# Attention stage of a two-layer decoder: one TensorE tile shape of 64 rows by 32 columns, two value banks, two score banks

## The reference

```
q = _layernorm(q, q_gamma, q_beta)
k = _layernorm(k, k_gamma, k_beta)
logits = jnp.einsum('bhsd,bhtd->bhst', q, k) / (math.sqrt(Dh) * T)
att = jax.nn.softmax(logits, axis=-1)
out = jnp.einsum('bhst,bhtd->bhsd', att, v)
```

## Time and profile before

| | |
|---|---|
| runs | 1680.69, 1681.13, 1683.37 us |
| median | 1681.13 us |
| span of the profiled execution | 1681.4 us (no other time of it is shown) |
| TensorE clock granted | mean 0.994 of full speed |
| busy: TensorE / VectorE / ScalarE / GpSimd | 1598.4 / 1499.6 / 1319.1 / 406.3 us |
| attention stage | about 130 to 1253 us of the span |

### The profile page before, as it was taken

The page is one execution under the profiler, slowest core; times in us unless marked ns, Lnnn a source line. Parts: engine busy times, 40 slices in busy tenths (PEclk is TensorE's granted clock), DMA queues, the critical chain, the costliest instruction groups (busy, mean ns, idle before and its releaser), DMA issues. The chain is left out here.

```text
span 1681.4 us, 36595 instructions
## 1 busy us (share of the span) xinstructions
PE 1598.4 (95%) x14449; PEld 634.1 (38%) x14452; DVE 1499.6 (89%) x2182; ACT 1319.1 (78%) x2590; POOL 406.3 (24%) x666
## 2 busy tenths in 40 slices
PE   6999999999999999999999999999989999889997
PEld 3542222222223232223322222222235555657774
DVE  6899999989999999989899999999948887688876
ACT  4618999879988989898899999999985565545544
POOL 5800110212223312312211111111013443533302
PEclk9999999999999999999999999999999999999999
DMA  4001001001101200101221011010002000015551
GB/s 147 14 7 20 14 14 14 14 14 22 31 14 21 45 14 14 33 17 27 70 55 26 14 21 20 14 27 14 14 28 63 1 1 1 1 31 95 101 102 51
DMA packets 148026, 52.32 MB, mean 31 GB/s; under 512 B 137424, under 2 KB 146128, under 8 KB 147600
## 3 DMA queue, kind: packets, MB, share of 16 engines
q1 hardware_dynamic: 147152, 48.62, 14.1%
q10 hardware_dynamic: 704, 1.38, 0.2%
HBM read 14.07 MB, written 2.10 MB: 10 GB/s over the span
## 5 line engine op out<-in xcount | busy, mean ns | idle before, releaser
L968 DVE TENSOR_REDUCE mxp<-ps_m 128x2 f32<-128x1024 f32 (+2 forms) x928 | 1049.3, 1198 | 41.3 <-PE ps_m L747 39.9
L897 ACT ACTIVATE work<-ps_s 128x512 f32<-128x512 f32 x1856 | 1001.7, 598 | 76.7 <-PE ps_s L771 48.9
L797 PE MATMUL ps_av<-work,vst 128*32 128x256 f32 x7424 | 592.8, 391 | 14.7 <-ACT avs L904 12.3
L771 PE MATMUL ps_s<-qb,k_stack 50*128 50x512 f16 x1856 | 565.8, 382 | 0.5 <-ACT v_rows L915 0.3
L747 PE MATMUL ps_m<-k_stack,qa 48*128 48x512 f16 (+1 forms) x2048 | 534.1, 358 | 2.3 <-PEq L1123 0.5
L797 PEld LDWEIGHTS ps_av<-work,vst 128*32 128x32 f32 x7424 | 147.0, 108 | 383.2 <-ACT work L897 321.6
L771 PEld LDWEIGHTS ps_s<-qb,k_stack 50*128 50x128 f16 x1856 | 119.7, 94 | 378.6 <-ACT work L897 323.4
L747 PEld LDWEIGHTS ps_m<-k_stack,qa 48*128 48x128 f16 x2048 | 108.2, 93 | 21.5 <-DVE mxp L968 14.8
L616 POOL TENSOR_SCALAR mtmp<-negm 128x16 f32<-128x16 f32 x32 | 8.2, 255 | 390.5 <-DVE negm L973 390.4
L602 POOL COPY vst<-v_rows 128x1024 f32<-128x1024 f32 (+1 forms) x32 | 30.6, 956 | 144.5 <-PE ps_av L797 144.5
L682 POOL TENSOR_TENSOR q_rows<-avs,rc 128x256 f32<-128x256 f32 x31 | 19.2, 619 | 173.3 <-DVE rc L979 173.3
(11 more groups left out here) (441 smaller groups left out, 2006.1 us busy)
## 6 DMA issues: line engine op xcount, KB each, us to landing
x_res<-in_x SPq DMA_DIRECT2D x4, 512.0 KB, 8.2
w_experts<-in_w_experts SPq DMA_DIRECT2D x1, 2048.0 KB, 8.0
out<-x_res SPq DMA_DIRECT2D x8, 256.0 KB, 2.2
v_rows<-in_ctx_c SPq DMA_DIRECT2D x1, 1664.0 KB, 7.3
work<-in_ctx_t SPq DMA_DIRECT2D x1, 1456.0 KB, 15.8
ctx_n<-in_ctx_n SPq DMA_DIRECT2D x1, 1248.0 KB, 8.0
w_qkv<-in_w_qkv ACTq DMA_DIRECT2D x1, 768.0 KB, 8.6
w_qkv<-in_w_qkv SPq DMA_DIRECT2D x1, 768.0 KB, 4.2
```

The costliest lines, as they stand in the source:

```text
L771: pe.matmul(ps_s[:, bank, :], STACKS[part(n)][rows, group(n) * PAIRS + j, t * P:t * P + P], qb[n % 2][rows, :, j, :], start=True, stop=Tru ...
L797: m = pe.matmul(ps_av[32 * h:32 * h + 32, cols], vst[n % 2][:, t, h, :], pbuf[(tau[n] + t) % 2][:, h, cols], start=(t == 0 and half == 0), ...
L897: a.activation(pbuf[g % 2][:, h, :], ps_s[:, b, :], ACT.Exp, scale=factor).then_inc(s["exp"], 1)
L968: v.tensor_reduce(dst, src, AX.X, ALU.max).then_inc(s["mred"], 1)
```

## The change

Scores, maxima and values all use tiles of 64 rows by 32 columns. A score is four matmuls with 32 keys each; a side of a maximum unit is four with 32 queries each; a value product is split into keys 0 to 63 and 64 to 127 (`side`), which go to two banks of `ps_av`. `collect` copies both banks (1024 columns) to `raw`, which lies in the same memory as `spare`, and a new step of GpSimd, `add_sides`, adds them before the transposes. PSUM has 8 banks, so the second value bank takes one of the score banks: `BANKS_S` is 2.

The order on TensorE changes too: in a half-step both sides of the maximum come before the second score, and the values of the turn before stand at its end (`half_step`). Values of a chunk's turn 0 are held back until the second half-step of turn 1, both halves together. The results of the chunk before come at turn 3 instead of 2, after its first half-step; ScalarE copies them after two exponentials; the row tiles move one turn back.

```diff
@@ -38,8 +38,9 @@
 AHEAD = 3
-BANKS_S = 3
+BANKS_S = 2
 HALF = 64
+QUARTER = [slice(c, c + 32) for c in range(0, P, 32)]
 MAXROWS = 3 * HD
@@ -381,12 +382,12 @@
-    SETTLE = 2
+    SETTLE = 3
     KEY_TURNS = [(6, 13)] + [(n, t) for n in (7, 10, 11, 14) for t in (4, 8, 12)]
     s = {k: fresh(prog, k) for k in ("set", "mx", "mred", "negm", "msplit", "sc", "exp", "vst", "av",
-                                     "avev", "rc", "norm", "kpeak", "kmax", "diag", "chain", "kh", "kl", "kset", "st", "ln", "pw", "xr", "late", "wchain", "ctx",
+                                     "avev", "rc", "norm", "sum", "kpeak", "kmax", "diag", "chain", "kh", "kl", "kset", "st", "ln", "pw", "xr", "late", "wchain", "ctx",
                                      "qb_in", "k_in")}
@@ -411,7 +412,7 @@
     def o_tile(n, t):
-        return n - GROUPS + t - 4 if settled(n) and 4 <= t < 4 + QC else None
+        return n - GROUPS + t - 5 if settled(n) and 5 <= t < 5 + QC else None
@@ -459,6 +460,17 @@
         return [unit_of(g) for g in range(lo, mid)], [unit_of(g) for g in range(mid, hi)]
+    def before(n, t):
+        if t > 0:
+            return n, t - 1
+        return (n - 1, keys_of(n - 1) - 1) if n > 0 else None
+    def halves_behind(t, j):
+        if t == 1:
+            return () if j == 0 else (0, 1)
+        return (j,)
@@ -468,12 +480,12 @@
         for t in range(keys_of(n)):
+            head, tail = coming(n, t)
+            made += len(head)
+            units += PAIRS
             if t == SETTLE and n > 0:
                 result_at[n - 1] = units
-            head, tail = coming(n, t)
-            made += len(head)
-            units += PAIRS
             for at_, tile in ((o_at, o_tile(n, t)), (x_at, x_tile(n, t))):
@@ -503,7 +515,7 @@
         mtmp = sb("mtmp", [P, NU], F32)
-        avs = sb("avs", [P, QC, P], F32)
+        avs, raw = sb("avs", [P, QC, P], F32), spare[:, :, :].rearrange("p s (a b) -> p s a b", b=P)
         rc = [sb(f"rc{p}", [P, QC, HG], F32) for p in range(2)]
@@ -517,7 +529,7 @@
         ps_m = cx.enter_context(nc.psum_tensor(f"ps_m{prog['n']}", [P, 2, 2, 512], F32))
-        ps_av = cx.enter_context(nc.psum_tensor(f"ps_av{prog['n']}", [P, 512], F32))
+        ps_av = cx.enter_context(nc.psum_tensor(f"ps_av{prog['n']}", [P, 2, 512], F32))
         block = cx.enter_context(nc.Block())
@@ -676,6 +688,11 @@
+            def add_sides(n):
+                g.wait_ge(s["avev"], n + 1)
+                g.tensor_tensor(raw[:, 0, :, :], raw[:, 0, :, :], raw[:, 1, :, :], ALU.add).then_inc(s["sum"], 1)
             def normalise(n):
@@ -691,6 +708,7 @@
                 if n > 0:
+                    add_sides(n - 1)
                     normalise(n - 1)
@@ -707,6 +725,7 @@
                     roots(n // GROUPS - 1, c)
+            add_sides(NCH - 1)
@@ -742,11 +761,11 @@
-                g = part(n)
+                g, rows = part(n), slice(e * HALF, e * HALF + MAXROWS)
                 for a, j, key, width, col in pieces(g, u):
-                    m = pe.matmul(ps_m[:, b, e, col:col + width], qa[n % 3][e * HALF:e * HALF + MAXROWS, a, j, :],
-                                  STACKS[g][e * HALF:e * HALF + MAXROWS, group(n) * PAIRS + j, key:key + width],
-                                  start=True, stop=True)
+                    for q in QUARTER:
+                        m = pe.matmul(ps_m[q, b, e, col:col + width], qa[n % 3][rows, a, j, q],
+                                      STACKS[g][rows, group(n) * PAIRS + j, key:key + width], start=True, stop=True)
                 return m
@@ -768,20 +787,24 @@
                 bank, rows = take_s(), slice(e * HALF, e * HALF + ROWS)
-                pe.matmul(ps_s[:, bank, :], STACKS[part(n)][rows, group(n) * PAIRS + j, t * P:t * P + P], qb[n % 2][rows, :, j, :],
-                          start=True, stop=True).then_inc(s["sc"], 1)
+                for q in QUARTER:
+                    m = pe.matmul(ps_s[q, bank, :], STACKS[part(n)][rows, group(n) * PAIRS + j, t * P + q.start:t * P + q.stop],
+                                  qb[n % 2][rows, :, j, :], start=True, stop=True)
+                m.then_inc(s["sc"], 1)
                 if j == PAIRS - 1 and e == 1:
-            def score(n, t, j, units):
+            def half_step(n, t, j, units):
                     max_side(*units[0], b, 1)
+                    max_side(*units[0], b, 0).then_inc(s["mx"], 1)
                 score_side(n, t, j, 1)
-                if units:
-                    max_side(*units[0], b, 0).then_inc(s["mx"], 1)
+                for half in halves_behind(t, j):
+                    if n > 0 or t > 0:
+                        values(*before(n, t), half)
                 for unit in units[1:]:
@@ -792,25 +815,21 @@
                         pe.wait_ge(s["avev"], n)
-                cols, end = slice(half * 256, half * 256 + 256), t == keys_of(n) - 1
-                for h in range(HG):
-                    m = pe.matmul(ps_av[32 * h:32 * h + 32, cols], vst[n % 2][:, t, h, :], pbuf[(tau[n] + t) % 2][:, h, cols],
-                                  start=(t == 0 and half == 0), stop=(end and half == 1))
+                cols = slice(half * 256, half * 256 + 256)
+                for side in range(2):
+                    keys = slice(side * HALF, side * HALF + HALF)
+                    for h in range(HG):
+                        m = pe.matmul(ps_av[32 * h:32 * h + 32, side, cols], vst[n % 2][keys, t, h, :], pbuf[(tau[n] + t) % 2][keys, h, cols],
+                                      start=(t == 0 and half == 0), stop=(t == keys_of(n) - 1 and half == 1))
                 m.then_inc(s["av"], 1)
-            def values_behind(n, t, half):
-                if t > 0:
-                    values(n, t - 1, half)
-                elif n > 0:
-                    values(n - 1, keys_of(n - 1) - 1, half)
-
             def results(n):
-                pe.wait_ge(s["avev"], n + 1)
+                pe.wait_ge(s["sum"], n + 1)
                 last = n == NCH - 1
                 for a in range(QC):
-                    m = pe.transpose(dst[:, a * P:a * P + P], avs[:, a, :], ident[:, :])
+                    m = pe.transpose(dst[:, a * P:a * P + P], raw[:, 0, a, :], ident[:, :])
                 m.then_inc(s["mx"] if last else s["sc"], 1)
@@ -832,15 +851,15 @@
                 if g < DENSE:
-                    idle_products(pe, ps_av[:, :], identh[:, :], qa[0][:, 0:2, :, :].rearrange("p a j b -> p (a j b)"), 2)
+                    idle_products(pe, ps_av[:, 0, :], identh[:, :], qa[0][:, 0:2, :, :].rearrange("p a j b -> p (a j b)"), 2)
                 for quarter in QUARTERS[g * len(QUARTERS) // EARLY:(g + 1) * len(QUARTERS) // EARLY]:
                     head, tail = coming(n, t)
+                    half_step(n, t, 0, head)
                     if t == SETTLE and n > 0:
                         results(n - 1)
-                    score(n, t, 0, head)
                     if o_tile(n, t) is not None:
@@ -869,11 +888,9 @@
                         pe.matmul(ps_m[:, b, 0, 0:2], ones[0:2, :], wdiag[:, :], start=True, stop=True).then_inc(s["mx"], 1)
-                    values_behind(n, t, 0)
-                    score(n, t, 1, tail)
-                    values_behind(n, t, 1)
-            values(NCH - 1, keys_of(NCH - 1) - 1, 0)
-            values(NCH - 1, keys_of(NCH - 1) - 1, 1)
+                    half_step(n, t, 1, tail)
+            for half in range(2):
+                values(NCH - 1, keys_of(NCH - 1) - 1, half)
             results(NCH - 1)
@@ -899,12 +916,12 @@
                 a.wait_ge(s["av"], 2 * tau[n + 1])
+                a.copy(raw[:, :, :, :], ps_av[:, :, :].rearrange("p s (a b) -> p s a b", b=P)).then_inc(s["avev"], 1)
+            def result(n):
                 if n > 0:
                     a.wait_ge(s["norm"], n)
-                a.copy(avs[:, :, :], ps_av[:, :].rearrange("p (a b) -> p a b", b=P)).then_inc(s["avev"], 1)
-
-            def result():
-
                 a.copy(avs[:, :, :], ps_s[:, bank(), :].rearrange("p (a b) -> p a b", b=P)).then_inc(s["exp"], 1)
@@ -927,10 +944,10 @@
                 for t in range(keys_of(n)):
-                    if t == SETTLE and n > 0:
-                        result()
                     weights(n, t, 0, factor)
                     weights(n, t, 1, factor)
+                    if t == SETTLE and n > 0:
+                        result(n - 1)
                     if o_tile(n, t) is not None:
```

2 lines of the change are left out of this document (1 added, 1 removed).

## The result

| | before | changed |
|---|---|---|
| median of the runs (4 each) | 1681.75 us | 1717.43 us (1716.09 to 1719.81) |
| ratio, 95% interval | | 1.0214 [1.0199, 1.0228] |
| span of the profiled execution | 1681.4 us | 1714.3 us (its time: 1716.09) |

The change makes the kernel 2.1% slower. The forecast was 1702, +21 us; it is +36 between the medians, and +33 between the two profiled spans, which is what a trace can explain.

The account below looks back on a forecast made before the run. VectorE and TensorE were taken as within 2% of each other, the two-bank loop then deciding. Cross 8.5, self 1, row tiles 9, last chunk 1 and end 1.9 gave +21 on 1681.1: 1702 us, range 1690 to 1722.

Parts of the forecast that it names:

- One tile shape: On TensorE, one shape for scores, maxima and values: its half-step falls from 1.11 to 0.93 us if undisturbed.
- Issue: TensorE's 32 matmuls and 32 loads per half-step: tiles taken to start 7 ns apart, against 0.047 us each as rival.
- The loop of two banks: A score bank's cycle, exponential to next exponential: 1.10 us per half-step, so TensorE's 0.18 is nearly all waited away.
- The seam: Between chunks: copy 0.78, held back values 0.32, result 0.84, together 1.9 us lost, 0.9 more than before.
- 13 plain cross chunks: Plain cross-attention chunks: 30.5 us against 29.85, +0.65 each, 8.5 us in all.
- 9 plain self chunks: Plain self-attention chunks: 37.3 us against 37.2, VectorE idling 0.6; +0.1 each, 1 us in all.
- 8 chunks with row tiles: Chunks with row tiles: a turn of 3.75 us against 3.66, four per chunk; +1.1 each, 9 us in all.
- First chunk: The first chunk has no seam, so nothing was added there: 0.
- The end: At the end nothing covers the wider copy and the addition: 0.43 + 1.46 = 1.9 us.

Follow-up runs that it names:

- short_exponentials: The changed kernel with each exponential covering only 256 of its 512 columns, both halves of a value product reading these; 1653.40 us, ratio 0.9828 to the changed kernel.
- banks2_alone: The kernel before with two score banks instead of three, old tile shapes and old order; 1795.76 us, ratio 1.0681.
- side0_three_banks: The changed kernel with only values of keys 0 to 63, one value bank, three score banks; 1666.87 us, 1756.87 profiled, at a falling clock.
- narrow_copy: The changed kernel with ScalarE copying only one value bank, 512 columns, and GpSimd adding that copy to itself; 1703.98 us.
- short_units_whole: The changed kernel with units of 65 columns left whole, not split in four column tiles; 1718.89 us, ratio 1.0213 to the kernel before.
- values_ahead_of_rows: The kernel before with one line moved: in row-tile turns the first half of the values stands ahead of the row tile; 1674.37 us, ratio 0.9956.

## Why the prediction was right, and where its sizes were off

**One tile shape** (0.93 per half-step): right, and a little too long; short_exponentials shows 0.88 or less.

**Issue** (7 ns per tile): right. The tiles of a group start 3 to 7 ns apart; in short_exponentials 32 matmuls and as many loads start in 0.88, and 12 more matmuls in the old order cost about 0.02.

**The loop of two banks** (1.10): exact. It was put together from four rows, and moves by the hundredth with the exponential (0.88 with one of 0.38). That TensorE's 0.2 per half-step bring nothing because of the loop is shown from both sides: banks2_alone takes the bank and nothing else, side0_three_banks gives it back, and short_exponentials shortens the loop without it.

**The seam** (1.9): of the right kind, 0.3 short. The copy's 0.78 came out as worked out, and narrow_copy gives its double width alone 0.43 per seam. The held back values cost 0.38 for 0.32. The result cost 0.93 for 0.84, as the four transposes start only when the values have drained; and small pieces of 0.15 weren't in the sum.

**13 plain cross chunks** (+8.5, measured +16.4): the term that was mis-sized. The undisturbed ones take 30.81 for 30.5: 13 x 0.96 = 12.5. Another 3.6 is scatter above 30.81, of which 2.3 lie in the four chunks with a stop of the kind described under short_units_whole. The last 0.4 is chunk 30, which was shorter before (29.46). No row of the kernel before shows such a stop, since its instructions landed long ahead; a program with more than twice as many instructions in this stage was a risk of its own, and the prediction weighed only the rate of starts, not their supply.

**9 plain self chunks** (+1, measured +5.5): also mis-sized. I let VectorE's work cover half of the seam. But nothing of a seam was covered, as narrow_copy shows: 0.44 less in self chunks too. With half-steps of 1.10 against its 1.13 VectorE doesn't lag far enough; that is worked out, not tried. Here is such a chunk of the changed kernel:

```profile
204.36:242.11 37.75, 36.28 (x1036) 15.89 (x1029) 36.87 (x35) 36.67 (x68) 5.11 (x9) 1.00 0.09 18
```

VectorE idles 0.88 of 37.75, not 0.6, and its own work takes 36.87 for 36.68.

**8 chunks with row tiles** (+9, measured +5.3): here the new order pays back. The turn takes 2.48 + 1.10 = 3.58, not 3.75: the transposes start after 1.25, as worked out (1.22), but from there to the next score pass 1.24 and not 1.43, because behind the values the projection follows the transposes sooner. In the old shapes that order alone is the 6.4 us of values_ahead_of_rows.

**First chunk** (0, measured +1.7): the clock, below. **The end** (+1.9, measured +3.0): in the stage itself right, since from the last exponential to the last reciprocal, which waits for the results, pass 4.94 instead of 3.18 (the copy took 0.43 more, the addition 1.26). The other 1.2 lie behind the stage, where the program is the same, and where this stretch differs by more than that from one profile to another (430.6 before, 427.2 in values_ahead_of_rows).

The sum was +21 against +33 in the spans: the cross chunks' term was too small by 7.9 and the self chunks' by 4.5, the row tiles' too large by 3.7, and the clock was missing. So the direction and the cause were right, the size was about 40% short, and it was luck that the row tiles took back some of the misses. The remaining 3 us up to +36 lie between executions; the profiled one was the shortest of its four.

## What to carry to other kernels

A resource that is used in turn (a PSUM bank) has a loop time: fill, wait, empty, release. Add it up from the timeline before giving one away; if the engine's own pace gets shorter than that loop, its gain is worth nothing, and each stall stays, since nothing can catch up. To find the loop count which instruction overwrites the bank of which, and put long work between the two, not behind them. And take a change that comes out at zero or worse apart: here one line of its new order was worth 0.4%, under the loss of the rest.
